# Self-attention ahead of a decoder kernel, rebuilt: keys and values of all rounds first, scores in pairs of batches, values block-diagonal, constant rows by DMA

## The reference

```python
q, k, v = xn @ Wq.T + bq, xn @ Wk.T, xn @ Wv.T + bv      # scaled, split into heads
for it in range(3):
    ql, kl, vl = qcur @ Wlq.T + blq, kcur @ Wlk.T + blk, vcur @ Wlv.T + blv
    qs, ks = _ln(ql, lnc_w) * tscale, _ln(kl, lnd_w)      # over the 16 values of a head
    ai = softmax(qs @ ks.T * sm_scale) @ vl
    qcur = qcur + ai
    kcur, vcur = kl, vl                                   # keys and values never see the output
```

## Time and profile before

| | before |
|---|---|
| median of 3 runs | 1876.13 us (1870.21 to 1881.58) |
| the profiled execution | 1873.4 us, span 1871.6 us, mean granted clock 0.945 |
| TensorE matmul busy | 1671.0 us (89%) |
| VectorE busy | 1250.4 us (67%) |
| ScalarE busy | 1072.1 us (57%) |
| GpSimd busy | 186.1 us (10%) |

### The profile page before, as it was taken

How to read it: one execution, slowest core, us unless ns; L and a number is a source line. 1 busy time by engine, 2 the same in 40 slices (tenths; PEclk the granted TensorE clock), 3 DMA queues, 4 the chain that set the end, 5 groups by cost and what they waited for, 6 DMA issues and landing times. The chain is left out here.

```text
span 1871.6 us, 25293 instructions
## 1 busy us (share of the span) xinstructions
PE 1671.0 (89%) x9566; PEld 629.1 (34%) x9566; DVE 1250.4 (67%) x1802; ACT 1072.1 (57%) x2079; POOL 186.1 (10%) x146
## 2 busy tenths in 40 slices
PE   5655469899999999999999999999999999999975
PEld 3434023133323333333333333333233333333232
DVE  4332767677777786777777867787778767776422
ACT  2221046666666666666666666666666666666650
POOL 6611010001000110011000100010001100000000
PEclk9665579999999999999999999999999999999998
DMA  3330170705152333416150706070614223240000
GB/s 103 73 57 20 40 142 23 125 21 97 42 102 47 76 74 72 76 38 104 51 98 8 127 23 127 22 120 29 110 38 85 65 46 56 51 52 1 4 23 14
DMA packets 99578, 115.93 MB, mean 62 GB/s; under 512 B 20729, under 2 KB 84986, under 8 KB 99458
## 3 DMA queue, kind: packets, MB, share of 16 engines
q1 hardware_dynamic: 96722, 113.27, 30.5%
q10 hardware_dynamic: 2736, 1.06, 0.2%
HBM read 79.51 MB, written 34.77 MB: 61 GB/s over the span
## 5 line engine op out<-in xcount | busy, mean ns | idle before, releaser
L960 ACT ACTIVATE xprobs<-banks 128x512 f32<-128x512 f32 x1664 | 902.8, 595 | 486.4 <-PE banks L847 470.9
L1148 DVE TENSOR_REDUCE xneg_max_pieces<-banks 128x2 f32<-128x1024 f32 x768 | 912.5, 1218 | 240.0 <-PE banks L824 236.7
L847 PE MATMUL banks<-xq_stacks,xk_stacks 99*128 99x512 bf16 (+1 forms) x1664 | 526.5, 386 | 36.8 <-ACT xprobs L960 23.1
L864 PE MATMUL values<-xprobs,xv_rows 128*17 128x512 f32 x3328 | 439.9, 600 | 1.0 <-ACT xprobs L960 1.0
L847 PEld LDWEIGHTS banks<-xq_stacks,xk_stacks 99*128 99x128 bf16 (+1 forms) x1664 | 127.9, 97 | 621.9 <-ACT xprobs L960 508.2
L824 PE MATMUL banks<-xk_stacks,xq_stacks 49*128 49x512 bf16 (+1 forms) x2048 | 257.5, 342 | 28.0 <-DVE xneg_max_pieces L1148 17.5
L1213 POOL TENSOR_TENSOR xk_parts<-xk_rest,xk_parts 128x401 bf16<-128x401 f32 (+1 forms) x64 | 59.8, 937 | 715.3 <-ACT xk_parts L925 715.0
L824 PEld LDWEIGHTS banks<-xk_stacks,xq_stacks 49*128 49x128 bf16 x2048 | 57.8, 95 | 167.2 <-issue 111.3
L1083 DVE TENSOR_TENSOR xk_rest<-work,xk_parts 128x401 f32<-128x401 f32 (+1 forms) x64 | 36.8, 576 | 93.7 <-PE work L732 63.8
L864 PEld LDWEIGHTS values<-xprobs,xv_rows 128*17 128x17 f32 x3328 | 56.0, 95 | 125.9 <-ACT xprobs L960 89.1
L1208 POOL TENSOR_TENSOR xrstd<-xrstd,mhalf 128x4 f32<-128x4 f32 x24 | 24.2, 1010 | 656.2 <-DVE xrstd L1020 656.2
(11 more groups left out here) (218 smaller groups left out, 1179.1 us busy)
## 6 DMA issues: line engine op xcount, KB each, us to landing
xk_stacks<-key_parts_dram SPq DMA_DIRECT2D x192, 200.1 KB, 12.3
key_parts_dram<-xk_parts SPq DMA_DIRECT2D x144, 100.0 KB, 1.7
xq_stacks<-parts_dram SPq DMA_DIRECT2D x192, 64.0 KB, 8.1
ctxT_a<-in_ctxT SPq DMA_DIRECT2D x4, 1601.0 KB, 7.5
ctxT_b<-in_ctxT SPq DMA_DIRECT2D x4, 1601.0 KB, 7.0
parts_dram<-xq_parts SPq DMA_DIRECT2D x48, 128.0 KB, 1.7
key_parts_dram<-xk_parts SPq DMA_DIRECT2D x48, 100.2 KB, 6.5
xa<-in_x SPq DMA_DIRECT2D x8, 512.0 KB, 14.6
```

The costliest lines, as they stand in the source:

```text
L847: pe.matmul(scores[n % SRING], kst[0:ROWS[par], k, h2, par, t * P:(t + 1) * P], qst[0:ROWS[par], k, h2, par, :], start=True, stop=True).th ...
L864: last = pe.matmul(av[32 * j:32 * j + HD + 1, :], vals[:, k, t, gr * GH + j, :], probs[:, sl % 2, j, :], start=t == 0, stop=t == XKT - 1)
L960: nc.scalar.activation(probs[:, sl % 2, j, :], scores[n % SRING], ACT.Exp).then_inc(exped, 1)
L1148: nc.vector.tensor_reduce(nmp[:, of % 2, j2, :, q, piece], pairs[n % MRING][:, :, :], AX.X, ALU.max, negate=True).then_inc(mxr, 1)
```

## The change

All keys and all values depend on the input alone. The changed kernel makes the centred keys of all three rounds first (`keys`, `next_values`), and variances as sums over heads by matmul. Keys are normed by a root that is spread over the partitions (`spread_roots`), queries are not: their root multiplies the scores. A score row holds the keys of two batches (`PAIR`, 32 tokens) for 16 heads, 512 columns instead of 2048, written in four matmuls of 32 output partitions. One exponential and four transposes follow. `values_by_head` makes values for a pair in four copies, one for each 32 partitions, of which VectorE keeps the diagonal (`vbd`), so that 16 matmuls give the output of all heads. GpSimd no longer fills the constant rows of `kst` and `qst`; ten DMAs bring them from a small array in memory. One `kproj` stands before round one and one in each round; the other four, the values and the gram blocks stand after the rounds, the last two kinds among the score pairs. GpSimd's queue, SP's queue and the order of jobs change with it.

```diff
+        root(rk[:, 0, :], 3)
+        root(rq[:], 4)
+        keys_by_head(0, 1)
+        root(rk_rest, 5)
+        beside("pool", 0)
+        for c in range(CH):
+            keys_by_head(1, c)
+        root(rq[:], 6)
+        beside("pool", 1)
+        for c in range(CH):
+            keys_by_head(2, c)
+        beside("pool", 2)
+        root(rq[:], 7)
...
+            act.wait_ge(exp_ready, it + 1)
+            a.activation(pr, pr, ACT.Exp).then_inc(exp_in, 1)
+            beside("act", it + 1)
+            act.wait_ge(pT_made, it + 1)
+            a.activation(pT, av[:].rearrange("p (k t) -> p k t", t=TOK), ACT.Copy).then_inc(pT_in, 1)
+            beside("act later", it + 1)
+            if it == 1:
+                act.wait_ge(diff_ready, 1)
+                a.activation(adiff[:], adiff[:], ACT.Abs, accum_out=asum[:]).then_inc(asum_ready, 1)
...
+        def score(it):
+            if it == 0:
+                pe.wait_ge(hide_in, 1)
+                pe.wait_ge(ks_in, 1)
+            pe.matmul(bank[0], ident[:], hidep[:].unsqueeze(1).broadcast_to([P, H, PAIR]), start=True, stop=False)
+            pe.wait_ge(cq_in, it + 1)
+            pe.wait_ge(ksM_in, CH * (it + 1))
+            for c in range(CH):
+                for n in range(PAIRS):
+                    tok = slice(n * PAIR, (n + 1) * PAIR)
+                    last = pe.matmul(bank[0][tok, c * HC * PAIR:(c + 1) * HC * PAIR], cq[:, c, tok], ksM[it][:, c, :, tok],
+                                     start=False, stop=c == CH - 1)
+            last.then_inc(sc_made, 1)
+
+        def values_by_head(it):
+            if it == 0:
+                pe.wait_ge(ck_in, ITERS)
+                pe.wait_ge(vn_in, ITERS - 1)
+            else:
+                pe.wait_ge(vb_in, it)
+            for n in range(PAIRS):
+                for c in range(CH):
+                    at = (n % 2 * CH + c) * P
+                    for i in range(QUAD):
+                        last = pe.matmul(bank[3 + n // 2][i * PAIR:(i + 1) * PAIR, at:at + P],
+                                         vT[it][:, c, n * PAIR:(n + 1) * PAIR], wl[:, 2, :], start=True, stop=True)
...
+        keys(0)
+        queries(0)
+        next_values(1)
+        key_vars(0)
+        query_vars(0)
+        keys(1)
+        next_values(2)
+        keys(2)
+        key_vars(1)
+        key_vars(2)
+        values_by_head(0)
+        beside("pe", 0)
+        spread_roots(0)
         for it in range(ITERS):
+            score(it)
+            if it < ITERS - 1:
+                values_by_head(it + 1)
+            beside("pe", it + 1)
+            pe.wait_ge(exp_in, it + 1)
+            transposes(av, [pr[:, k * P:(k + 1) * P] for k in range(QUADS)]).then_inc(pT_made, 1)
+            if it == 0:
+                spread_roots(1)
+                spread_roots(2)
+            pe.wait_ge(pT_in, it + 1)
+            pe.wait_ge(vb_in, it + 1)
+            for k in range(QUADS):
+                for n in range(PAIRS):
+                    tok = slice(n * PAIR, (n + 1) * PAIR)
+                    last = pe.matmul(bank[2][tok, k * QUAD * HD:(k + 1) * QUAD * HD], pT[:, k, tok], vbd[it][:, n, k, :],
                                      start=True, stop=True)
...
+        def query_vars(it):
+            pe.wait_ge(sqq_in, it + 1)
+            by_head(bank[1][:, D:D + H], sqq).then_inc(vq_made, 1)
...
+        key_normed(0)
+        dve.wait_ge(ks_in, 1)
+        v.tensor_tensor(ksM[0][:, 0, :, :], ck[:, 0, 0, :].unsqueeze(1).broadcast_to([P, HC, TOK]),
+                        head[:].unsqueeze(2).broadcast_to([P, HC, TOK]), ALU.mult).then_inc(ksM_in, 1)
+        values_by_head(0)
...
+            dve.wait_ge(sc_made, it + 1)
+            link(v.tensor_reduce(mx[:], sc3, AX.X, ALU.max))
+            link(v.tensor_tensor(pr3, sc3, mx[:].unsqueeze(2).broadcast_to([TOK, H, PAIR]), ALU.subtract))
+            dve.wait_ge(root_ready, (4, 6, 7)[it])
+            v.tensor_tensor(pr3, pr3, rq[:].unsqueeze(2).broadcast_to([TOK, H, PAIR]), ALU.mult).then_inc(exp_ready, 1)
+            if it == ITERS - 2:
+                dve.wait_ge(stored, 16)
+            if it < ITERS - 1:
+                values_by_head(it + 1)
+            if it == 0:
+                key_roots_wide(1, ITERS, 5)
+            beside("dve", it + 1)
...
+            link(v.tensor_reduce(rsum[:], pr3, AX.X, ALU.add))
...
-        FIRST_KEYS = [[("kproj", i, 0) for i in one] for one in (range(0, 3), range(3, 6), range(6, 2 * NP))]
-        FIRST_VALUES = [[("v", 4, 0), ("v", 5, 0)], [("v", 6, 0), ("v", 7, 0)],
-                        [("wdT", 0, 0), ("wdT", 1, 0)] + [("gw", i, 0) for i in range(NPAIR)]]
-        AFTER = [("x1T", 0, 0), ("x1T", 1, 0), ("qproj", 0, 0), ("max", 0, 0), ("qproj", 1, 0)]
-        FIRST = Phase(True, [j for it in range(ITERS) for j in FIRST_KEYS[it] + FIRST_VALUES[it]] + AFTER)
+        BESIDE = [[("kproj", i, 0)] for i in range(ITERS + 1)]
+        AFTER = [("kproj", 4, 0), ("x1T", 0, 0), ("x1T", 1, 0), ("qproj", 0, 0), *[("kproj", i, 0) for i in (5, 6, 7)]]
+        AMONG_PAIRS = {2: ("v", 4, 0), 4: ("v", 5, 0), 6: ("v", 6, 0), 8: ("v", 7, 0), 10: ("wdT", 0, 0),
+                       12: ("wdT", 1, 0), **{14 + 2 * i: ("gw", i, 0) for i in range(NPAIR)}}
...
+                sp.wait_ge(flat_stored, 16)
+                for c in range(CH):
+                    for dst, one in ((kst[49:51, c, :, 0, :], 0), (kst[48:64, c, :, 1, :], 0), (qst[48:49, c, :, 0, :], 0),
+                                     (qst[112:113, c, :, 1, :], 0), (qst[50:64, c, :, 1, :], 1)):
+                        rows, n = dst.shape[0], dst.shape[-1]
+                        sp.dma_start(dst, g.flat_dram[one:one + 1, 0:n].unsqueeze(1).broadcast_to([rows, HP, n])
+                                     ).then_inc(flat_in, 16)
+            elif what == "stacks":
+                for i in range(2):
+                    sp_key_parts(i, i)
+            elif what == "x":
...
                 sp.dma_start(xa[:], g.x[0].rearrange("(q p) d -> p q d", p=P)).then_inc(x_in, 16)
+                sp_key_parts(2, 2)
+            elif what == "decoder":
+                sp.dma_start(wdec, g.Wdec.rearrange("(i e) h d -> (e h) i d", e=2)).then_inc(loaded, 16)
+                sp_key_parts(3, 3)
+                sp_key_parts_out(1)
+                sp_key_stacks(0, 0, True)
+                sp_key_stacks(0, 0, False)
...
+            if what == 2:
                 pool.wait_ge(x_in, 16)
                 pool.wait_ge(loaded, N_LOADS)
+                p.tensor_tensor(xa[:], xa[:], bo[:].unsqueeze(1).broadcast_to([P, QT, D]), ALU.add).then_inc(sum_ready, 1)
...
+                sp_key_parts(4, 4)
                 sp_query_parts(0, 0)
-                sp.wait_ge(zeroed, 14)
                 sp.wait_ge(qparts_out, 48)
                 sp_query_stacks(0, True)
                 sp_query_stacks(0, False)
+                for i in range(5, 2 * NP):
+                    sp_key_parts(i, i)
...
+                    if n in AMONG_PAIRS:
+                        dve_job(FIRST, AMONG_PAIRS[n])
```

718 lines of the change are left out of this document (415 added, 303 removed).

## The result

The changed kernel takes 1796.14 us as the median of four runs (1792.98 to 1798.67), the kernel before 1878.35 us in four runs beside them. The ratio is 0.9568, with a 95% interval of 0.9532 to 0.9603; five further runs of it gave 0.9579 (0.9551 to 0.9607). The forecast was 1809 us with a range of 1790 to 1835, so the time lies in the range and 13 us under the forecast. The profiled execution took 1795.9 us, with a span of 1793.8 us, against 1871.6 before.

The account below looks back on a forecast made before the run. The front was taken as a chain of engines waiting for each other. Preamble -0.7, rounds 52.6, to output 22.8, bridge 2.1 and pairs -12.3 sum to 64.5 us, from 1873.4 to 1809 us, range 1790 to 1835.

Parts of the forecast that it names:

- the rounds: First to third exponential: two rounds take 39.5 us instead of 92.1, a gain of 52.6 us.
- the pairs: Stage of score pairs: ten jobs move in and lengthen VectorE's path, a loss of about 12 us, 12.3 in the sum.
- The price of the tiled products: In each round: values by head 4.2 us (bounds 2 and 16.6), probabilities times values 1.6 us (bounds 1 and 7.0).
- The first rival: Column-tiled products in the rounds do not run side by side: 1843 to 1877 us, about 1855; chance 0.10.
- The root behind the decoder weights: Second round: third round's query root, behind an addition waiting for all weights, comes 1.7 us after VectorE wants it.
- Preamble, output, bridge: First exponential at 43.5 us; third exponential to output 5.0 us, gain 22.8; output to first pair 28.8 us, gain 2.1.
- a transfer takes the gain: Root waits behind decoder weights, or query stacks behind keys: 11 us more, about 1820, up to 1830; chance 0.12.
- Constant rows: GpSimd's long fills go, but no engine of the chain waited for them; ten transfers replace them: nothing gained.
- Tiling modes: Alternating tiled and whole matmuls four times a round may drain TensorE; a drain of 0.2 us makes the sum 2.4 us worse.
- Shorter still: Rounds at 2.4 GHz take 16 us each, pairs 8 us more than before, key stacks still 21: 1790 to 1797; chance 0.10.

Follow-up runs that it names:

- run with fills: Changed kernel with the constant rows of key and query stacks filled by GpSimd again in place of the ten DMAs: 1820.99 us, ratio 0.9702.
- run with tiles apart: Changed kernel with loops of the column-tiled products reordered so neighbouring products go to the same group of 32 columns: 1811.02 us, ratio 0.9648.
- root first: Changed kernel with GpSimd's addition of bo moved behind the root of the third round's queries: 1797.76 us, ratio 0.9581.
- jobs ahead: Changed kernel with the ten small weight jobs among the first batch's pairs all run before the first pair: 1810.81 us, ratio 0.9647.
- run with keys and values in the rounds: Changed kernel with keys of rounds two and three made in the round before, and round three's values there too: 1809.01 us, ratio 0.9639.

## Why the prediction came out as it did

The mechanism was right: a chain of waits in the front is shortened, with a main stage that keeps its length (within 0.1 us between the two main profiles, within 3 us over all variants). Two terms of the sum were mis-sized, both on the side of caution: the rounds, by 6.8 us, and the pairs, by 7.2.

- **The price of the tiled products.** The step "I take a quarter of 0.26 us: 4.2 us" for the values by head measured 1.92 us, under its lower bound of 2, and "1.6" for the output measured 0.65. That is 3.2 us in each of the two rounds, 6.5 of the term's 6.8. The quarter was right, and the clock was not. The 0.26 us are from L326, which ran at a granted clock of 0.50; in the changed kernel both groups met 1.00. At that clock whole instructions of 128 columns start 0.11 us apart (four of L377 every 0.45 us, 21.09 to 22.43), and a quarter of this is 0.028 where 0.030 was measured; the output's instructions cost 0.020. The forecast's bound "2 us (the same at 2.4 GHz)" is this case. In the run with fills the values by head of the second round met a clock of 0.50 and took 3.67 us, near the 4.2:

```profile
70.67 3.67 PE L443 MATMUL banks<-s_wl,xa 128*32 128x128 f32 x64
```

```profile
70.67:74.34 3.67, 3.67 (x69) 3.29 (x61) 2.11 (x3) 0.63 (x1) 3.61 (x3) 0.50 0.11 32
```

  The first rival (not side by side) is excluded by the run with tiles apart, which also shows the size of what hung on it: 13.4 us of span, 11.6 of them in the front, not the 34 to 68 of that rival. The scores keep their speed there, the output slows by a factor of two, and the values by three, to 0.093 us an instruction.
- **The root behind the decoder weights.** The step "the root comes 1.7 us after VectorE wants it" did not occur. The weights landed by 68.57, where I had assumed 76.5, and the root was 0.95 us early; with the root first nothing changed. That is 1.7 us more of gain in the second round.
- **VectorE beside GpSimd.** The sum had no such term. The trace of before had the sign of it, which I passed over: in its VectorE timeline a product of 512 columns takes 1.41 us, with GpSimd at work from 27.44 to 30.53, where its like takes 0.69. Neither of its operands is in the matmul banks, and this holds for L658 and L633 too.

```profile
28.38 1.41 DVE L431 TENSOR_TENSOR err<-err,s_vars 128x512 f32<-128x512 f32 x1
```

  L658 and L633 cost 1.08 and 0.61 us more than their like, 1.7 us in the first round. So the periods were 18.0 and 14.7 us, where 19.5 and 20.0 were forecast: 19.5 less 3.2 plus 1.7, and 20.0 less 3.2 less 1.7, leave 0.4 us unexplained in the second. This sum takes in the largest differences alone; smaller ones partly cancel in it, as the key projection (1.61 us against 2.4) and mask with scores (3.8 against 3.3).
- **The pairs.** The step "1.2 to 3.2 us each for three", and 1.1 for a gram job, took VectorE to wait for TensorE at each. It does not. VectorE's busy time rises from 39.1 to 43.5 us, the rest of the stage from 8.7 to 9.3. A value job costs its copy, 0.68 us (0.28 for the short one), and a gram job 0.73 (two pairs of small operations), 5.2 us in all; the stage is 5.1 us longer than before and 4.9 us longer than with the jobs ahead of it, and not 12. The granted clock is 0.65 there instead of 0.54, with TensorE busy for 35.6 us of the stage instead of 23.5.
- **Preamble, output, bridge.** 43.5 against 42.8, 5.0 against 5.6, 28.8 against 29.5 us. The bridge's mechanism held too: key stacks first, query parts behind them, the first pair released by the query stacks. The stacks ended at about 104 and the parts landed at 105.6, both 6 us ahead of the forecast, as the start of the output was 7 us ahead. The rival "a transfer takes the gain" was in the forecast itself, as the small gain of the bridge. By itself, without that queue, the forecast had the bridge 25 us long, and with half of the key stacks moved behind it was 25.9.
- **Constant rows.** "Nothing gained" is right for the old order and wrong as a statement on the change. The product of keys by head and the roots of the queries moved onto GpSimd's queue, behind the place of the fills. Had the fills stayed, they would have cost 23.5 us. The sum came out right there only because both were changed together.
- **Tiling modes.** The Trainium skill, "TensorEngine Tiling (Array Packing)", section Tiling Modes, has a change of mode drain TensorE. The trace shows no cost that could be put to it: the tiled L443 starts at 57.75, behind the tiled L429 that ends at 57.92, and both follow whole matmuls in every round. No run here measured a drain by itself.
- **Shorter still** had 0.10 with 1790 to 1797, on the condition that the rounds run at 2.4 GHz. The time is that of this rival, and lies just outside the 1798 to 1820 that had 0.65. Its condition held in part: the granted clock was 0.81 and 0.65 over the two rounds, 1.00 from 57.75 to 59.67 and from 61.47 to 63.46, with the values by head, the transposes and the output, but 0.52 from 50.97 to 57.92, with the queries, the variances and the scores. The rounds took 32.7 us together, near its twice 16. Its other term was off, since the pairs lost not 8 us but 5.

## What to carry to other kernels

When a helper engine gets a link of the chain, everything that stands ahead of it in its queue becomes part of the chain, so a fill that was free must be costed again in the new order. Small jobs among reductions cost the reducing engine its own time and little more, as long as TensorE has slack; as a chain of their own they cost 18.3 us instead of 4.9. Products for different column groups should be issued in turn, group after group: the same 64 instructions took 1.9 or 5.9 us by the order of the loops, with eight products in a row on one group in the slow order. A price taken from a row belongs to the granted clock of that row: these 64 instructions took 1.92 us at 1.00 and 3.67 at 0.50.

## What the runs showed of the hardware that was not expected

- 64 float32 instructions of 128 columns with 32 output columns each took 1.92 us in turn over the four groups and 5.93 us in runs on one group. For 16 of 256 columns, with two products in a row on a group, the order made no difference (1.07 and 1.09 us).
- VectorE's addition L658 of 256 columns took 0.42 us alone and 1.50 us beside GpSimd's products of 1024 columns, and a square of 256 columns 0.42 and 1.70 us. Beside the same products, operations that read one operand from the matmul banks kept their time: L655 at 48.02 and L663 at 50.50 with 0.42 us, L631 at 58.73 with 0.69. Beside GpSimd's fills, in the run with fills, the addition took 0.42 us, and beside a GpSimd root the product L633 took 0.69 us at 42.03.
- It goes the other way too: VectorE's product of 1024 columns L620, which starts at 36.33, takes 1.22 us, and GpSimd's like product, which starts 0.05 us later, takes 2.93 us, where two of them take 3.74 in the run with keys and values in the rounds.
- A GpSimd root costs by its width: 2.91 us for 16 values a row, 5.42 for 32.
